# Twelve shared blocks ahead of the expert pairs, and routed results laid by their place among a token's experts

## The reference

```python
probs = softmax(xt @ w_router)                      # xt: 2048 x 256, 16 experts
top_w, top_i = top_k(probs, 4); top_w /= sum(top_w)
g = silu(einsum('td,edh->teh', xt, we1)) * einsum('td,edh->teh', xt, we3)   # h = 128
moe_out = einsum('teh,ehd->td', g * cw[:, :, None], we2)
shared = silu(xt @ ws1) * (xt @ ws3) @ ws2          # hidden 512
out = shared / 5 + moe_out * 4 / 5
x = x + gb * out
```

## Time and profile before

| | |
|---|---|
| median of 3 runs | 380.18 us |
| profiled execution, its span | 380.9 us |
| TensorE busy with matmuls | 329.5 us (87%) |
| VectorE, ScalarE, GpSimd busy | 258.2, 197.8, 213.2 us |
| DMA | 56.36 MB, mean 148 GB/s |

### The profile page before, as it was taken

How to read it: one execution, slowest core, us unless ns; L and a number is a source line. 1 busy time by engine, 2 the same in 40 slices (tenths; PEclk the granted TensorE clock), 3 DMA queues, 4 the chain that set the end, 5 groups by cost and what they waited for, 6 DMA issues and landing times.

```text
span 380.9 us, 8085 instructions
## 1 busy us (share of the span) xinstructions
PE 329.5 (87%) x2296; PEld 305.0 (80%) x2296; DVE 258.2 (68%) x720; ACT 197.8 (52%) x436; POOL 213.2 (56%) x289
## 2 busy tenths in 40 slices
PE   3986997997888999999890399999999998999890
PEld 1676997997887899898770389999999998988770
DVE  1888895578985886757891379656656555516996
ACT  2456666465675656746340078656666665621100
POOL 1486563333388887757777007766666666651240
PEclk9999897799999999999997589999999999999997
DMA  6346500000011229982232346666675666239952
GB/s 217 115 148 203 166 28 16 8 20 14 3 62 70 79 92 316 305 271 111 108 126 108 95 98 183 186 184 201 174 207 166 197 187 175 91 91 412 409 191 83
DMA packets 54554, 56.36 MB, mean 148 GB/s; under 512 B 17424, under 2 KB 46864, under 8 KB 54512
## 3 DMA queue, kind: packets, MB, share of 16 engines
q1 hardware_dynamic: 46560, 34.21, 30.6%
q0 software_dynamic: 6864, 19.80, 13.7%
q10 hardware_dynamic: 1088, 1.84, 1.4%
HBM read 31.43 MB, written 24.40 MB: 147 GB/s over the span
## 4 chain that ended last, share of the span: by engine, by line
PE 44%; POOL 13%; DVE 11%; DMA 10%; issue 9%; SPq 8%; ACT 3%; DVEq 0%; POOLq 0%; ACTq 0%
PE ps L1540 11%; PE ps L1541 11%; PE ps L1542 11%; POOL xg_rows L631 7%; DMA y_in<-y_rows 4%; SPq L523 3%; PE ps L1863 3%; SPq L518 3%; POOL y_rows L658 2%; DMA x_in<-in_L_attn_x_dram 2%; DMA xs<-xg_rows 2%; PE ps L1694 1%; PE ps L1896 1%; POOL rstd L598 1%; PE ps L1633 1%
## 5 line engine op out<-in xcount | busy, mean ns | idle before, releaser
L658 POOL DMA_INDIRECT y_rows<-y_sb,aside x79 | 76.5, 969 | 53.0 <-ACT y_sb L930 38.9
L631 POOL DMA_INDIRECT xg_rows<-hrow,slot_u x64 | 66.3, 1037 | 20.7 <-issue 18.9
L1540 PE MATMUL ps<-rpool 128*128 128x256 f32 (+3 forms) x228 | 70.8, 311 | 6.3 <-DVE rpool L1060 6.2
L1541 PE MATMUL ps<-rpool 128*128 128x256 f32 (+3 forms) x228 | 67.8, 297 | 0.0
L1542 PE MATMUL ps<-rpool 128*128 128x256 f32 (+3 forms) x228 | 67.7, 297 | 0.0
L1540 PEld LDWEIGHTS ps<-rpool 128*128 128x128 f32 x228 | 45.5, 200 | 8.9 <-DVE rpool L1060 8.3
L1540 PE MATMUL ps<-w_hi_routed,xT_hi 128*128 x158 | 45.8, 290 | 2.2 <-DVE xT_lo L1469 2.1
L1542 PEld LDWEIGHTS ps<-rpool 128*128 128x128 f32 x228 | 45.5, 199 | 0.6
L1541 PEld LDWEIGHTS ps<-rpool 128*128 128x128 f32 x228 | 45.5, 200 | 0.5
L1542 PE MATMUL ps<-w_hi_routed,xT_lo 128*128 x158 | 45.2, 286 | 0.0
L1541 PE MATMUL ps<-w_lo_routed,xT_hi 128*128 x158 | 45.2, 286 | 0.0
(11 more groups left out here) (208 smaller groups left out, 893.4 us busy)
## 6 DMA issues: line engine op xcount, KB each, us to landing
xs<-xg_rows SPq DMA_DIRECT2D x79, 128.0 KB
y_in<-y_rows SPq DMA_DIRECT2D x8, 1024.0 KB, 12.1
xg_rows<-empty SPq DMA_DIRECT2D x1, 2304.0 KB, 8.2
x_in<-in_L_attn_x_dram SPq DMA_DIRECT2D x16, 128.0 KB, 2.1
w_raw_routed<-in_L_ffn_we_dram SPq DMA_DIRECT2D x8, 256.0 KB, 3.8
out_dram<-x SPq DMA_DIRECT2D x16, 128.0 KB, 2.4
wmod_sb<-in_L_wmod_dram ACTq DMA_DIRECT2D x3, 512.0 KB, 7.4
w_raw_routed<-in_L_ffn_we_dram SPq DMA_DIRECT2D x4, 320.0 KB, 7.0
```

The costliest lines, as they stand in the source:

```text
L631: nc.gpsimd.indirect_dma_start(out=xg, out_offset=bass.IndirectOffsetOnAxis(ap=slot_u[:, t, k:k + 1].bitcast(U32), axis=0), in_=hrow[:, t, ...
L658: nc.gpsimd.indirect_dma_start(out=yb, out_offset=bass.IndirectOffsetOnAxis(ap=dest[:, 2 * n + i:2 * n + i + 1].bitcast(U32), axis=0), in_ ...
L1540: nc.tensor.matmul(dst, w[0], x_[0], start=first, stop=False)
L1541: nc.tensor.matmul(dst, w[0], x_[1], start=False, stop=False)
```

## The change

- `UNITS_FIRST` goes from 8 to 12: units 8 to 11 are done ahead of the pairs, units 12 to 15 behind them. All 16 experts are split ahead of the pairs, and the first pair waits for them.
- `shared_out` writes the gated result to a buffer in SBUF (`gated`), in two halves, and not back to PSUM. `down` of the next block's first unit waits for these halves, and no longer for the addition to `x1`.
- The result of a token's k-th expert (k from 0 to 3) goes to row (1 + k) * 2048 + token. A "place" k is thus a stretch of 2 MB. It is loaded by 4 DMAs of 512 KB, one for each block, with runs of 1 KB.
- SyncE does not wait for all sends: `route_marks` on VectorE counts, for each place, how many sends of each ring slot must have landed. Place k holds nothing from experts above 12 + k. SyncE reads these counts from SBUF (16 `value_load`s) and waits for them place by place.
- The additions are per place and block of 512 tokens (`add_place`, 128x1024). For the last block GpSimd adds places 2 and 3 (`JOINED`). GpSimd adds 7 of 8 half blocks to `x1` (6 before). The last block's shared part is added at the very end (`last_shared`, `last_rows`).
- GpSimd gets five small instructions for the constants of `route_marks`, ahead of the last 32 sends.

```diff
-UNITS_FIRST = 8
-SPLIT_FIRST = 10
+UNITS_FIRST = 12
-ADDED_BY_POOL = HALVES - 2
+ADDED_BY_POOL = HALVES - 1
+JOINED = (3,)
@@ sync, behind the pairs' loop
-            for r in range(RING):
-                sp.wait_ge(s_back[r], 16 * loads_of(NPAIR - RING + r))
-            for b in range(NB):
-                for half in range(2):
-                    first = 1 + (b * BT + half * BT // 2) * P * TOPK
-                    rows = slice(half * BT // 2, (half + 1) * BT // 2)
-                    sp.dma_start(y_in[b][:, rows], yb[first:first + BT // 2 * P * TOPK, :].rearrange(
-                        "(t p k) d -> p t k d", p=P, k=TOPK)).then_inc(s_yin[2 * b + half], 16)
+            sp.wait_ge(s_marks, 1)
+            for k in range(TOPK):
+                counts = [sp.value_load(marks[0:1, k, r:r + 1], min_val=32, max_val=16 * loads_of(NPAIR - RING + r))
+                          for r in range(RING)]
+                for r in range(RING):
+                    sp.wait_ge(s_back[r], counts[r])
+                for b in range(NB):
+                    first = (1 + k) * T + b * TB
+                    sp.dma_start(whole(b)[k], yb[first:first + TB, :].rearrange("(t p) d -> p t d", p=P)
+                                 ).then_inc(s_yin[k][b], 16)
@@ gpsimd
+            done(pool, "scores", TILES - 1)
+            nc.gpsimd.iota(first_of[:, 0, :]...
+            for r in range(RING):
+                nc.gpsimd.memset(sent_all[:, :, r:r + 1], 16.0 * loads_of(NPAIR - RING + r)).then_inc(s_mark_const, 1)
             send(TILES * TOPK - sent[0])
...
+            for b in JOINED:
+                y = whole(b)
+                pool.wait_ge(s_yin[2][b], 16)
+                pool.wait_ge(s_yin[3][b], 16)
+                nc.gpsimd.tensor_tensor(y[2], y[2], y[3], ALU.add).then_inc(s_joined, 1)
             for j in range(ADDED_BY_POOL):
                 y, mine = part(j)
                 pool.wait_ge(s_scaled, j + 1)
-                nc.gpsimd.tensor_tensor(mine, mine, y[:, :, 0, :], ALU.add).then_inc(s_done_p, 1)
+                nc.gpsimd.tensor_tensor(mine, mine, y[0], ALU.add).then_inc(s_done_p, 1)
@@ scalar and vector, ahead of the pairs
-            splits = {..., 7: [8, 9]}
+            splits = {..., 7: [8, 9], 8: [10, 11], 9: [12], 10: [13, 14], 11: [15]}
@@ vector
+            def route_marks():
+                last = tb[:, 2, E - TOPK:E].rearrange("p (k n) -> p k n", n=1)
+                ...begun = (last > first_of); passed = sum over the pairs of a ring slot
+                marks = min(32 * passed, sent_all)
@@ vector, shared_out(b)
-                nc.vector.tensor_tensor(out_ps, out_ps, gate_, ALU.mult).then_inc(s_gated, 1)
+                for i in range(2):
+                    nc.vector.tensor_tensor(gated[:, i * BT // 2:(i + 1) * BT // 2, :],
+                                            ps[:, 4 + i, :].rearrange("p (t d) -> p t d", d=D), gate_, ALU.mult
+                                            ).then_inc(s_gated, 1)
@@ vector, the tail
+            for b in range(NB):
+                add_place(b, 1)
+            add_place(0, 2)
+            add_place(1, 2)
+            g_step(UNITS_FIRST)
+            add_place(0, 3)
+            scale(0)
+            scale(1)
+            g_step(UNITS_FIRST + 1)
+            add_place(1, 3)
+            scale(2)
+            scale(3)
+            g_step(UNITS_FIRST + 2)
+            add_place(2, 2)
+            add_place(2, 3)
+            scale(4)
+            scale(5)
+            g_step(UNITS_FIRST + 3)
+            add_place(3, 2)
+            scale(6)
+            scale(7)
+            finish(HALVES - 1)
+            last_shared(0)
+            last_shared(1)
+            last_rows(0)
+            last_rows(1)
@@ tensor, down(n)
-                if e == 0 and b > 0:
-                    if b > UNITS_FIRST // SH:
-                        pe.wait_ge(s_added, 2 * (b - UNITS_FIRST // SH))
-                    else:
-                        pe.wait_ge(s_shared, b)
                 if n == UNITS_FIRST:
                     pe.wait_ge(s_ry, NPAIR)
                 for j in range(BT):
+                    if e == 0 and b > 0 and j % 2 == 0:
+                        pe.wait_ge(s_gated, 2 * (b - 1) + j // 2 + 1)
```

174 lines of the change are left out of this document (91 added, 83 removed).

## The result

| | before | after |
|---|---|---|
| median, us | 380.1 (20 runs) | 384.3 (20 runs) |
| ratio after / before | | 1.0071, 95% interval 1.0041 to 1.010 |
| profiled execution, span in us | 380.9 | 386.9 |

The change makes the kernel slower by 0.7%: within 1%, but 10.5 us away from the predicted 373.8 and outside the range of 367.5 to 380.

The account below looks back on a forecast made before the run. No engine bounds the whole; two seams count, TensorE's idle ahead of the pairs and the tail set by VectorE. 347.2 + 17.0 + 7.7, with 2.6 for the store, gave 374.5; less 0.7, median 373.8, range 367.5 to 380.

Parts of the forecast that it names:

- Part 1: Ahead of the pairs: four units and six splits moved there leave TensorE no gap; all pair times move by -0.5 us.
- Part 2: Result loads behind the pairs: issued once SyncE is free, at 370 GB/s; block 0 of place 3 lands at 347.2.
- Part 3: VectorE's tail from 347.2: 17.0 us of work plus 7.7 lost beside GpSimd, ending at 371.9.
- port rival: VectorE's tail: GpSimd's additions exclude VectorE's wholly, 11.6 us lost, 377.7 in all; chance 0.14.
- little contention: Tail: loads at 404 GB/s and only 0.3 us lost for each GpSimd addition, 367.1 in all; chance 0.15.
- Full first seam: Ahead of the pairs: slower steps or stretched sends start pairs 3.5 to 5.8 us later, 377 to 380; chance 0.12.
- failed start: Behind the pairs: counts hold SyncE until the last send, bytes flow at 342.9, 387.9 in all; chance 0.07.
- (a): Ahead of the pairs: TensorE idles below 1.5 us before the first transpose, clock 1.00, pair 4's transposes near 224.7.
- (c): Tail: block 0 of place 3 lands near 347; VectorE waiting for DMA beyond 350 means slower 1 KB runs than taken.
- (d): Tail: VectorE's additions of 1.23 us take 1.9 to 2.5 beside GpSimd.
- (b): Behind the pairs: the first place load is issued at 322 to 325; at 340 it is the failed start.
- (e): End of the kernel: VectorE ends near 372 while TensorE ended before 365.

Follow-up runs that it names:

- the five edits: Changed kernel with TensorE's register loads at block 9, count reads ahead of sends, 4 KB runs, places 2/3 block by block, no GpSimd adds: 370.6 us, ratio 0.9736.

## Why the prediction was wrong

By the ruler the span of after's second profile is 10.1 us over the sum (the first gives 10.3):

| term | us |
|---|---|
| twelve blocks end later (48.85 instead of 47.5) | +1.35 |
| register loads behind them | +1.83 |
| pair 0 to pair 4, clock behind the gap (10.6, taken as 9.7) | +0.9 (first profile +3.3) |
| pair 4 to SyncE's end of the pairs | +0.7 |
| reads ahead of the first load (2.6, taken as 1) | +1.6 |
| first load to block 0 of place 3 (27.2, taken as 24.0) | +3.2 |
| VectorE's tail (24.06, taken as 24.7) | -0.6 |
| stores (3.85, taken as 2.6) | +1.2 |

**Part 1, the step that failed first.** "TensorE now has no gap": it has one. The three register loads stood in the 13.75 us of idle, where they cost nothing; the step filled this cover and did not ask what else had lain in it. 1.83 us for three is 0.61 each, as SyncE's reads show too. That moving them removes the gap is shown (four profiles). The clock fell in all eight profiles on the usual chips that kept the gap and in none of the four that did not (three here, one on the other chip); but it stayed up with the gap in the run without early start on the other chip: a gap makes the fall likely, not certain. The forecast that without a gap pair 4 comes at +9.7 is met where rows were in time (9.37), not here (10.8), since TensorE waited for rows and the sends were late; so the clock alone, kept up, brought nothing here (10.8 against 10.6). (By its own 47.5 + 9.7 pair 4 comes at 225.2; the 224.7 in the list of signs is a slip.)

The "1 us for all" on the sends was 2.8. The prediction saw one stretched send (1.63) and did not count how many of the 32 would begin within a split or an addition: eight, by the rule above, where before it was two. The Trainium skill (SBUF — State Buffer, "Who interferes with whom") says that a DMA which seems stalled by VectorE is one whose descriptors GpSimd writes, for want of the port pair that the two share. The trace agrees: 0.96 us alone, 1.43 to 1.72 when begun within VectorE's instruction. But the same place tells of a probe in which `tensor_tensor` did not stall a DMA; here all eight long sends begin within one, and the measurement decides.

The blocks themselves were 0.17 us late at the start of `gate_up(11)` and 0.4 at its end; the three last products, taken at 1.5, took 5.35 / 3 = 1.78.

**Part 2.** The counts and what they allow were right: the first load was issued as soon as SyncE was free and had read its counts, and without the early start the kernel took 14.8 us more. The read was at the end of its range or just over it (0.3 to 2.5 for four; 2.5 to 2.6 measured), not at the 1 taken. The rate was the larger miss: 370 GB/s taken within 335 to 404, while 1 KB runs alone moved 348 at a share of 1.10. Divided by the share, as the prediction did with its rows, this is 316, below its lower end. That rate alone is 2.1 us by the experiment; and the reads and it are not two terms but one behind the first load. The Trainium skill (DMA: Bandwidth & Descriptors, "Why small descriptors are slow (HBM only)") gives a fixed cost of about 3 cycles for each packet, one beat being 32 bytes; by this 1 KB takes 35 cycles where 4 KB takes 131, an estimate of 6.4% less rate. Measured was 348 against 417, 17% less: the trace does not agree in size.

**Part 3 was right in its mechanism, and in its sum partly by luck.** 17.0 of work and 7.7 of contention, 24.7, against 24.07 in every profile of the changed kernel; by the run without GpSimd it is 15.8 and 8.2, one too high by 1.2 and the other too low by 0.5. The port rival (11.6 lost) did not come about, little contention neither. But being right about a term is not to ask whether it need be there: without GpSimd it is 21.6.

**The rivals.** "Full first seam" (377 to 380) came nearest in mechanism: its place was right, its causes in part (the stretched sends, not a full VectorE at unit 9), its size too small by 4.3 us since it left the second seam alone. The failed start's 387.9 is 3.6 us off, but nothing of what it describes happened. That "little contention" and the forecast got 0.67 between them came from taking each unknown near its middle, while of eight terms seven came out on one side: each was a cost of a place where I had seen slack. Of the signs, (a) failed (1.83 us, clock down) and (c) too, in the way that it names: the 1 KB runs are slower than taken. (d) held in kind: the additions took 1.69 to 2.10 us there, the scales up to 2.83. (b) failed in its time, 161.5 to 162.7 from zero where it says 154 to 157, but the first load follows SyncE's last pair load and not the last send. (e) failed: VectorE ended some 9 us late, and TensorE ended at 208.7 to 208.9 from zero, where the sign says before 197; VectorE, with no idle of over 0.15 us in the tail, did not wait for it.

**What stays open.** Why the clock is down for three windows of 4 us behind the gap in three profiles of the eight (0.50 in the middle one, pair 4 at +12.8 to +13.0) and for two, at 0.70 to 0.88, in the other five. Of the stores' 1.2, some 0.4 are the last two half blocks' stores queueing (VectorE ends the two halves 0.6 us apart, before 1.3); the other 0.8 lies behind the landing of the last store (1.25 us to the end of the span, before 0.4) and isn't traced. What the six moved splits cost. A single register load of all 16 counts, which by 0.61 us for 16 values on TensorE would cost a sixteenth of the reads, was not tried.

## What to carry over

Before you fill a gap, list everything that stands in it, register loads, memsets and descriptor writing too: what was free there is on the path afterwards. When a load is started earlier, charge it for the engines' whole traffic in that time and for its run length, and look for the next thing that is late. And at the end of a kernel, try what one engine does alone before giving a second one a share.

## What the chip showed that I had not expected

- A register load costs 0.60 to 0.61 us on TensorE and on SyncE, whether it fetches 1 or 16 values (1.83 for three of 16; 10.1 for 17, 16 of them of one).
- With 128 runs of 4 KB a load takes 0.64 us to issue (5.1 for the first 8 of the five edits). With 512 runs of 1 KB 16 loads take 24.3 us to issue with nothing between them, 1.5 each, though the first three take 0.39 to 0.52: slow issue is a sign of outstanding transfers.
- Loads of 1 KB runs move 348 GB/s at a DMA share of 1.10, those of 4 KB runs 417 at 1.02.
- GpSimd and VectorE: an indirect send takes 0.96 us of GpSimd. Begun within a VectorE instruction with two SBUF inputs it takes what is left of that one plus 0.83; begun ahead of it, 0.96 still. A pair of scales takes 1.29 alone and 3.44 beside GpSimd's additions; six of these take 11.68 us, 1.95 each, 1.29 alone.
- The same kernel reaches one and the same send at 162.3 or at 170.1 us: 8 us, twice the effect of the change. And the pairs alone spread by 3.3 us. A stage can be read from one profile only against an event at its beginning.
